# The sum of the first layer's expert rows, moved into the second attention's block and shared between VectorE and GpSimd

## The reference, cut to what matters

```python
x = x + _L0_xattn_ref(_layernorm(x), ctx_2048, ...)
x = x + _L0_ffn_ref(_layernorm(x), ...)     # moe_out (two rows a token) + shared
x = x + _L1_xattn_ref(_layernorm(x), ctx_2048, mask_BxS2_ik0, ...)
x = x + _L1_ffn_ref(_layernorm(x), ...)     # four rows a token
```

## Time and profile before

| | us |
|---|---|
| median of 3 executions | 1764.74 |
| lowest, highest | 1764.31, 1765.02 |
| the profiled execution | 1765.31 |
| its span | 1763.6 |

### The profile page before, as it was taken

The page is one execution under the profiler, slowest core; times in us unless marked ns, Lnnn a source line. Parts: engine busy times, 40 slices in busy tenths (PEclk is TensorE's granted clock), DMA queues, the critical chain, the costliest instruction groups (busy, mean ns, idle before and its releaser), DMA issues. The chain is left out here.

```text
span 1763.6 us, 43951 instructions
## 1 busy us (share of the span) xinstructions
PE 1519.7 (86%) x14968; PEld 1227.8 (70%) x14968; DVE 1345.9 (76%) x2949; ACT 1079.1 (61%) x3276; POOL 1053.9 (60%) x1063
## 2 busy tenths in 40 slices
PE   4999999999999999988988841899988249999966
PEld 4888888888888888865657730466656149999955
DVE  3898998999999999976644546489987328888876
ACT  3888888888888888863325620666552036666610
POOL 2667676767666666654764750027777736666642
PEclk9999999999999999998998975899997569999989
DMA  6600000000000000003235653002222855555557
GB/s 178 182 20 20 18 13 20 20 20 20 20 20 20 14 17 20 17 2 134 83 133 170 198 163 132 13 25 83 95 71 81 283 191 166 167 165 163 168 196 282
DMA packets 103082, 167.67 MB, mean 95 GB/s; under 512 B 20223, under 2 KB 75980, under 8 KB 102480
## 3 DMA queue, kind: packets, MB, share of 16 engines
q1 hardware_dynamic: 77136, 105.37, 19.3%
q0 software_dynamic: 22272, 56.15, 8.6%
q10 hardware_dynamic: 3456, 3.34, 0.6%
HBM read 95.31 MB, written 75.76 MB: 97 GB/s over the span
## 5 line engine op out<-in xcount | busy, mean ns | idle before, releaser
L438 POOL TENSOR_TENSOR w_down<-w_down,attn_rsum 128x1024 f32<-128x1024 f32 x256 | 483.9, 1895 | 234.9 <-DVE attn_rsum L397 233.9
L366 ACT ACTIVATE w_down<-attn_ps_s,attn_negmax 128x256 f32<-128x256 f32 x1024 | 469.6, 499 | 1.8 <-DVE attn_negmax L391 1.8
L402 DVE COPY w_down<-attn_ps_t 128x1024 f32<-128x1024 f32 x256 | 312.1, 1219 | 40.2 <-PE attn_ps_t L288 36.5
L391 DVE TENSOR_REDUCE attn_negmax<-attn_ps_s 128x4 f32<-128x1024 f32 x256 | 309.5, 1209 | 41.8 <-PE attn_ps_s L276 41.4
L961 POOL DMA_INDIRECT l_by_token<-layer_arena x240 | 240.1, 1000 | 150.1 <-issue 99.1
L276 PE MATMUL attn_ps_s<-ctx_d,attn_q_sb 64*128 64x256 f32 x2048 | 280.2, 386 | 2.1 <-ACT w_down L366 1.4
L302 PE MATMUL attn_ps_qo<-w_down,attn_vb 128*64 128x256 f32 x2048 | 250.6, 386 | 1.6 <-DVE w_down L402 1.3
L366 ACT ACTIVATION_READ_ACCUMULATOR w_down<-attn_ps_s,attn_negmax 128x1 f32 x1024 | 239.1, 233 | 0.0
L1130 POOL DMA_INDIRECT l_rows_in<-layer_arena,l_routing_group_slots x192 | 190.4, 991 | 57.6 <-issue 43.0
L288 PEld LDWEIGHTS attn_ps_t<-ident,w_down 64*128 64x128 f32 x4096 | 168.4, 138 | 77.6 <-issue 71.5
L276 PEld LDWEIGHTS attn_ps_s<-ctx_d,attn_q_sb 64*128 64x128 f32 x2048 | 209.6, 189 | 5.8 <-issue 2.8
(11 more groups left out here) (208 smaller groups left out, 2403.3 us busy)
## 6 DMA issues: line engine op xcount, KB each, us to landing
layer_arena<-l_rows_in SPq DMA_DIRECT2D x240, 136.0 KB, 2.3
w_gu<-l_by_token SPq DMA_DIRECT2D x32, 512.0 KB, 10.3
ctx_d<-in_ctx SPq DMA_DIRECT2D x64, 128.0 KB, 2.8
layer_arena<-l_by_token SPq DMA_DIRECT2D x32, 256.0 KB, 3.8
w_gu<-in_w_gu SPq DMA_DIRECT2D x16, 512.0 KB, 4.7
l_rows_in<-zeros SPq DMA_DIRECT2D x1, 4352.0 KB, 37.5
x_sb<-in_x SPq DMA_DIRECT2D x32, 128.0 KB, 2.5
w_down<-in_w_down SPq DMA_DIRECT2D x1, 4096.0 KB, 12.4
```

Of the source, the lines that this page charges most:

```text
L366: last = nc.scalar.activation(prob[:, n % 4, c, :], ps_s[:, n % 2, c, :], ACT.Exp, bias=negmax[:, n % 2, c:c + 1], accum_out=sums[:, n % 2 ...
L391: nc.vector.tensor_reduce(negmax[:, n % 2, :], ps_s[:, n % 2, :, :], AX.X, ALU.max, negate=True).then_inc(max_ready, 1)
L402: nc.vector.tensor_copy(prob_t[:, n // 2 % 2, n % 2, :, :, :].rearrange("p k c (d s) -> p d (k c) s", d=2), ps_t[:, :, :, :].rearrange("p ...
L438: nc.gpsimd.tensor_tensor(prob[:, n % 4, :, :], prob[:, n % 4, :, :], rsum[:, n % 2, :].unsqueeze(2).to_broadcast([P, 4, A_N]), ALU.mult). ...
```

## The change

`combine0` is deleted. What is left of it in the first layer's block is SyncE's wait for `all_stored`. The sum is now made inside `attention1`, in place: the ring of eight places (`parts`) lies in the memory that `xf` uses later.

- SyncE issues the first eight loads of row pairs, then the context of groups 0 and 1, then the other 24 loads of row pairs, each as its place comes free, and then goes on as before.
- VectorE adds tiles 0 to 3 ahead of the statistics of group 0 and tiles 4 to 7 between these and the normalisation of group 0. Each tile is two adds of 128x256 f32 with a wait between them.
- GpSimd adds tiles 8 to 31: four after the deviations of groups 0 and 1, and four after each of its steps 0 to 4. Then it clears the tails of `xf`, which it did first before.
- New waits: VectorE waits for GpSimd's adds ahead of the statistics of groups 2 and later, and ahead of `apply_f`.

```diff
     @block.sync
-        load(0, 0)
-        load(0, 1)
+        def load_parts(t):
+            if t >= HELD:
+                if t - HELD < BY_DVE:
+                    sp.wait_ge(added_by_dve, t - HELD + 1)
+                else:
+                    sp.wait_ge(added_by_pool, t - HELD - BY_DVE + 1)
+            sp.dma_start(parts[:, t % HELD, :, :],
+                         before.by_token[t * P * 2:(t + 1) * P * 2, :].rearrange("(p k) h -> p k h", k=2))\
+              .then_inc(parts_loaded[t % HELD], 16)
+        for t in range(HELD):
+            load_parts(t)
+        load(0, 0)
+        load(0, 1)
+        for t in range(HELD, NT):
+            load_parts(t)
     @block.vector
+        def add_parts(t):
+            tile = x_sb[:, t, :]
+            dve.wait_ge(parts_loaded[t % HELD], 16)
+            nc.vector.tensor_tensor(parts[:, t, 0, :], parts[:, t, 0, :], parts[:, t, 1, :], ALU.add).then_inc(paired_by_dve, 1)
+            dve.wait_ge(paired_by_dve, t + 1)
+            nc.vector.tensor_tensor(tile, tile, parts[:, t, 0, :], ALU.add).then_inc(added_by_dve, 1)
         def apply_f(it, q):
+            dve.wait_ge(added_by_pool, NT - BY_DVE)
             if j == 2 and gexists(it, g + 2):
+                dve.wait_ge(added_by_pool, (g + 3) * GT - BY_DVE)
                 statistics(it, g + 2, stats_a, mv_a, vare_a, steps_a)
-        for q in range(2):
-            statistics(0, q, stats_a, mv_a, vare_a, steps_a)
-            apply_a(0, q)
+        for t in range(GT):
+            add_parts(t)
+        dve.wait_ge(added_by_dve, GT)
+        statistics(0, 0, stats_a, mv_a, vare_a, steps_a)
+        for t in range(GT, 2 * GT):
+            add_parts(t)
+        apply_a(0, 0)
+        dve.wait_ge(added_by_dve, 2 * GT)
+        statistics(0, 1, stats_a, mv_a, vare_a, steps_a)
+        apply_a(0, 1)
     @block.gpsimd
-        rt.clear_tails(pool, xf)
+        def add_parts(t):
+            tile, slot = x_sb[:, t, :], t % HELD
+            pool.wait_ge(parts_loaded[slot], 16 * (t // HELD + 1))
+            nc.gpsimd.tensor_tensor(parts[:, slot, 0, :], parts[:, slot, 0, :], parts[:, slot, 1, :], ALU.add)\
+                .then_inc(paired_by_pool, 1)
+            pool.wait_ge(paired_by_pool, t - BY_DVE + 1)
+            nc.gpsimd.tensor_tensor(tile, tile, parts[:, slot, 0, :], ALU.add).then_inc(added_by_pool, 1)
+        pool.wait_ge(added_by_dve, BY_DVE)
+        for t in range(BY_DVE, BY_DVE + GT):
+            add_parts(t)
         for r in range(FIRST + len(rounds)):
             step(0, r)
+            for t in range((r + 3) * GT, min((r + 4) * GT, NT)):
+                add_parts(t)
+            if (r + 4) * GT == NT:
+                pool.wait_ge(added_by_pool, NT - BY_DVE)
+                rt.clear_tails(pool, xf)
```

Here `HELD` is 8 and `BY_DVE` is 8. The program's end of the first layer reads:

```diff
                     all_stored = experts(stages, block, nc, sb, m0, w_gu0, w_down0, None, entered)
-                    combine0(stages, block, nc, sb, m0, all_stored)
+
+                    @block.sync
+                    def _(sp):
+                        all_stored(sp)
```

More of the change, by code:

```diff
@@ L1412, in norm_apply @@
     last.then_inc(xn_ready, 1)
[L1415 to L1446, removed]
 C_HEADS = 16
@@ L1452, with attention1 @@
 VW = C_DH + 1
-def attention1(stages, block, nc, ins, sb, m, w, region, later, later_written, written_before):
+def attention1(stages, block, nc, ins, sb, before, m, w, region, later, later_written, written_before):
     ph = Stage(stages, "attn1")
@@ L1474, in attention1 @@
     XF = Routing.RING
+    HELD, BY_DVE = 8, 2 * GT
+    first = ph.used[0]
     xf = ph.sbuf("xf", [P, XF, GT, RW])
+    parts = ph.arena[:, first:first + HELD * 2 * H].rearrange("p (d k n) -> p d k n", d=HELD, k=2)
     xt = ph.sbuf("xt", [P, KT, GN])
@@ L1514, in attention1 @@
      ct_copied, y_made, delta_ready, rstd_d_ready, xb_ready, scaled_ready, x_ready) = by_tile.values()
+    parts_loaded = [ph.sem(f"parts_loaded{n}") for n in range(HELD)]
+    paired_by_dve, added_by_dve = ph.sem("paired_by_dve"), ph.sem("added_by_dve")
+    paired_by_pool, added_by_pool = ph.sem("paired_by_pool"), ph.sem("added_by_pool")
     bank_made, bank_free = ph.sem("bank_made"), ph.sem("bank_free")
@@ L2202, in build_program @@
             with nc.Block() as block:
-                entered = attention1(stages, block, nc, ins, sb, m1, w1, w_gu1, weights, later_loaded, written + 16)
+                entered = attention1(stages, block, nc, ins, sb, m0, m1, w1, w_gu1, weights, later_loaded, written + 16)
                 all_stored = experts(stages, block, nc, sb, m1, w_gu1, w_down1, m1.block_bias, entered)
```

## The result

| | before | after |
|---|---|---|
| median, us | 1762.55 (8 executions, 1760.23 to 1765.02) | 1753.99 (8 executions, 1747.35 to 1758.89) |
| the profiled execution, us | 1765.31 | 1752.75 |
| its span, us | 1763.6 | 1750.9 |

The ratio of after to before is 0.9944, with an interval of 0.9927 to 0.9962. On the median that the prediction started from this makes 1764.74 x 0.9944 = 1754.9 us: a gain of 9.9 us (6.7 to 12.9), where 20.3 were forecast. The sign was right; the size was about half of the forecast, and 1753.99 lies 1 us beyond the upper end of the stated range. The two profiled executions are 12.6 us apart.

A forecast was written before the change was run, and what follows sets the result against it. combine0, a serial block holding other engines at the barrier, was the bound: 26.0 us gained at entry less 5.7 lost in GpSimd's late rounds makes 20.3, so 1764.74 becomes 1744.4, taken as 1744.5; own range 1741.5 to 1747.5, wide 1739 to 1753.

The forecast's parts named there:

- What bounds the kernel, and the removal: At the seam: combine0 is a serial block; without it the barrier starts and the entry moves 31.74 us earlier.
- VectorE's eight tiles: Adds before group 0's normalisation: 0.86 us a tile, 3.54 plus 2.21 us, together 5.75 us on the path.
- The start chain: From TensorE's first transposes to the first clipping on VectorE: the same chain with the same 27.5 us.
- SyncE's queue: Context loads behind row-pair loads stay hidden; groups 0 and 1 have a cover of over 10 us.
- GpSimd's rounds: Tiles 8 to 31 at 1.49 us each; first three rounds free with 20 us idle after, later ones lose 5.7 us.
- The lateness in steps 3 to 5: GpSimd's deviations reach VectorE's residual late by 1.1, then 3.1 more, 7.2 us in all before idle time absorbs some.
- rival B: GpSimd's rounds are dearer: at 1.9 us a tile 10.6 us lost, 1749.3 us; chance 0.20.
- Contention of the two engines: Small disturbance between GpSimd and VectorE; 0.15 us allowed for tiles 20 to 23 beside the normalisation.
- A: GpSimd's rounds cost almost nothing on the path, giving 1738.7 us; chance 0.13.
- D: Slower through GpSimd's rounds in steps 2 to 4: break-even 3.2 us more a tile, 1774 at 4 us; chance 0.03.
- C: Entry dearer by 3 to 6 us, through less barrier time for engines or TensorE's clock: 1747.5 to 1750.5; chance 0.08.

The follow-up runs named there:

- g4: Changed kernel plus one more GpSimd drain, 16 indirect transfers before the end of the first layer's scatter of expert rows; 1751.38 us in a single execution.
- e1: Changed kernel with the first layer's block ending without GpSimd's drain; 1797.96 us, ratio 0.9914 to the kernel before.
- g1: Kernel before the change, with the first layer's block ending without GpSimd's drain; 1764.69 us, ratio 0.9999.
- g2: Changed kernel, no GpSimd drain, GpSimd's rounds early, VectorE's work ahead of group 0's normalisation cut; 1733.23 us, ratio 0.9819 to the kernel before.
- e2: Changed kernel with all of GpSimd's add rounds run before its first deviation, none behind steps 2 to 4; 1796.26 us, ratio 0.9902 to before.
- e0: The changed kernel run again, unchanged, as base of the first set; 1804.77 us, ratio 0.9941 to the kernel before.
- e3: Changed kernel with both edits: no GpSimd drain at the block's end, all GpSimd rounds early; 1787.83 us, ratio 0.985 to before.
- g3: Changed kernel without GpSimd's drain, its rounds early except tiles 28 to 31 and the tail clearing behind step 4; 1737.08 us, ratio 0.9849 to before.

## Why the prediction was right and wrong

**What bounds the kernel, and the removal.** Right about `combine0`: a serial block. The step "The barrier starts at 1046.70 instead of 1078.44, so the whole entry moves forward by 31.74 us" is **the step that failed**. It took the 1.42 us between VectorE's last add and SyncE's load for the price of the barrier. That number held only while the last engine to arrive was VectorE. With `combine0` gone GpSimd is the last, and it arrives some 8 us after its last transfer (the 8.3 us worked out at g4). SyncE's first load was forecast at 1048.12 and came at 1055.64, 7.5 us late. e1 gives back 7.1 us of it, g1 shows why no row of before had it; most of the rest is that the last transfer ended 0.48 us later in the trace of after (1045.96 against 1045.48).

**VectorE's eight tiles.** Forecast 0.86 us for a tile, measured 1062.03 - 1061.23 = 0.80. Four tiles and the wait took 3.30 us (1061.23 to 1064.53) instead of 3.54, the second four 3.18 with the power hidden under them, as forecast. That is 0.5 us better than stated, and leaves the 7.0 us by which the first transposes missed 1064.3.

**The start chain.** Forecast 27.5 us, measured 27.47 (1071.30 to 1098.77).

**SyncE's queue.** Hidden, as forecast; no wait of TensorE for a context appears.

**GpSimd's rounds.** Price (forecast 1.49 us for a tile, measured 1.48), place and the 20 us of idle time after the first three are right, and so is the choice of `add_beta`'s row as the price. The lateness in steps 3 to 5 was forecast as 1.1, 3.1 and 3.0 us. The trace shows none, 2.36 and 2.82; in the first VectorE comes late itself, since its normalisations take 2.68 us beside GpSimd's adds instead of 1.79. The sum lost is 6.5 us (19.1 to 12.6) against 5.7 (the prediction's own 7.2 - 1.6 is 5.6). The missing 0.8 is contention, which the prediction had put at 0.15 us in one place on GpSimd and at nothing on VectorE. Counted from the first clipping, the deviation of tile 3 was forecast ready at 1132.8 - (1117.87 - 26) = 40.93 us and was ready at 1139.48 + 0.55 - 1098.77 = 41.26, 0.3 later, with single adds of GpSimd up to 0.91 us; the residual's first instruction behind it took 0.94 instead of 0.47, 0.5 more. That is dearer, as rival B has it, but B's price (10.6 us lost) did not come.

**Contention of the two engines.** Beside GpSimd's adds VectorE's L1840 took 0.94 us instead of 0.47, and two-operand adds in g2 0.95 instead of 0.42, while GpSimd's went from 0.72 to 0.80 to 0.91. None of these grew by more than 0.53 us, less than one of GpSimd's adds (0.72). Others kept their length beside the same adds: in the trace of after the clipping at 1128.63 took 1.22 us (1.22 in before) and `normalise` at 1126.81 (L1815) 0.42 (0.42 at 1144.04 in before). On VectorE the lengthened rows between the two clippings add up to about 3 us (the normalisations 0.9, the residuals of three steps 2.0). Most of that only took the place of waiting for GpSimd; 0.8 us reached the path.

**The rivals.** A (no loss) is refuted by e2: undoing the late rounds gives 7.1 us. B (dearer rounds) would have lost 10.6 us with 1.9 us for a tile; a tile took 1.48, and the largest loss between the two clippings in any trace is 8.4 us (g4). That the stated range reaches to 1753 counts on a B beyond its 1749.3, for which no run shows a price. D (slower) would have needed 3.2 us for a tile. **C, "the entry is dearer", is what happened**, at 7.0 us instead of its 3 to 6, and by a cause that it didn't name: it looked at engines other than GpSimd and at the clock. It had a chance of 0.08. Its priced end was 1750.5; forecast plus both misses, 1744.4 + 7.0 + 0.8 = 1752.2, is 0.6 us from the profiled 1752.75. That the time came so near the stated range is owed to the width of the range, which was made for A, B and C; a drain of 7 us was in none of them. The 12.6 us between the profiles lie within the interval of the ratio, near its end; its middle is 9.9.

**What stays open.** Executions of after spread by 11.5 us, those of before in the same set by 4.8; in the second set before spread by 14.4, so the spread is not the change's alone. The granted clock of an execution goes with it (after: 0.939 at 1758.89, 0.949 at 1747.35). What sets it was not tried. The two places where the traces show TensorE's clock to differ with the same code, the start chain and the steps behind the late rounds, are worth up to 4.0 and 1.9 us.

## What to carry to other kernels

When a block that every engine waits for is removed, ask of every engine when it would arrive at the barrier, not only of the one that arrives last now, and don't take an engine without rows in the trace for one that has arrived: GpSimd had 0.07 us of busy time in the 9.7 us ahead of the first load, and taking out its drain made them 2.5. Here that drain, after 144 indirect transfers, took 7 of the 26 us that the entry should have gained; to learn whether another kernel pays it, run it once without the drain, as e1 and g1 did. Then put moved work into the longest idle stretch whole: here 24 tiles fitted into a gap of which the change used half, and the rest cost 7 us in steps that had 3 to 4 us of room.

## What the runs showed of the hardware

- **GpSimd's drain after indirect transfers.** 7.8 us after 128 transfers (g4), about 8.3 after 144 (after), at most 1.5 after 16 (the 2.9 us above less 1.42): about 0.06 us each. It shows in no row of GpSimd, only as a gap ahead of its next instruction (8.13 us in g4) or as SyncE's wait at the barrier (7.4 us in after, 0.3 without it in e1).
- **The same matmuls at two clocks.** The four groups of q and k projections in the start chain take 3.4 to 3.8 us where the granted clock is 0.50 to 0.57 and 1.95 or 1.96 at 1.00, here in the trace of after:

```profile
1074.42:1078.20 3.78, 3.78 (x4) 1.17 (x4) 3.04 (x4) 0.00 (x0) 3.54 (x6) 0.50 0.24 72
1093.75:1095.71 1.96, 1.96 (x4) 0.65 (x4) 0.00 (x0) 0.00 (x0) 0.00 (x0) 1.00 0.55 134
```

  Of the four groups three were slow in before, after, e1 and g2, four in e0 and e2, two in e3, g1, g3 and g4, with TensorE waiting 0.87 to 4.5 us ahead of each group in all of them. One step is worth 1.8 us, and it moved the start chain between 25.4 and 29.4 us without any edit to it: about half of what e1 or e2 gains. A single time, or a start chain read from one trace, doesn't tell an edit of 2 us from this.
